# Edge blocks in pairs in the third and fifth segment of a round, and the root, scale and last step of y placed later

## The chip, the cores and the metric

The kernel runs on one core of a Trainium2 chip. The metric is the device time of one execution in microseconds, as the median of several runs. A core has five engines with an instruction queue each: TensorE (PE; its weight loads are shown apart as PEld), VectorE (DVE), ScalarE (ACT), GpSimd (POOL) and SyncE (SP), which here only issues transfers. They meet through semaphores.

## What is computed

A graph layer with 6,250 nodes, 206,250 edges and 128 features. The edges come sorted by their target node `dst`. Cut to what matters:

```python
h = x @ W_node.T + b_node
e = edge_attr @ W_edge.T + b_edge
msg = (h[src] + e) @ W_msg.T + b_msg
s = segment_sum(msg, dst)
y = x + s / max(deg, 1)
out = (y - mean(y)) / sqrt(var(y) + 1e-5)
```

Since all of it is linear up to the division, the kernel sums first and multiplies by the weights afterwards: for each node the sum of its edges' features and the sum of its sources' rows of x.

## The kernel before

**Two strands.** The first sums edge features. It reads `edge_attr` in 101 *blocks* of 2,048 edges (1 MB each) into three buffers `edges`. For a block TensorE multiplies one-hot rows of 32 relative targets with the edges (`sum_windows`, L545: 16 products of 128*32 tiles, each shown as two passes since it is f32, so 32 rows of the trace), which gives four windows of 32 nodes in `win_ps`. ScalarE copies them to `win_sb` (`copy_windows`, L1171), TensorE moves the four windows to their places with a product with `place` (`place_windows`, L552), and VectorE adds the result to `sums_e`, the sums of all nodes (`add_sums`, L744). `win_ps`, `win_sb` and `place` are double, `onehot` is threefold.

The second strand sums rows of x. For each of 25 groups of 250 nodes (a *round*) it counts how often each source occurs at each target. VectorE makes one-hot rows and keys (`make_hots`, L754), TensorE multiplies them (`count_fill`, L613), ScalarE moves the counts from three banks to `counts` (`move_bank`, L1227), and in the round after TensorE multiplies the counts with x, split in three bf16 parts (`apply_counts`, L628, 147 products a round).

**Slots, rounds, segments, fills.** All engines walk through the same 133 *slots*. The first 8 (the lead) hold one block each. Then come 25 rounds of 5 *segments*, each with 5 *fills* `f` = 0 to 4: on TensorE a fill is 5 count products and, from the second round on, some 6 products with x. The table `block_at` (L81 to L86) tells which block is summed in which slot: 93 blocks over the second to fifth segments of 25 rounds, one a segment at most. In a slot, TensorE does the block's windows first, then the fills, with the place product behind fill 1. VectorE makes the next segment's one-hots first, then adds the block of this segment, and makes `place` for the next block and `onehot` for the block after it. ScalarE copies the block's windows first and then moves the five banks.

**Finishing a group.** Two rounds after a group's counts were made, in the first segment of a round (`finish_at`), TensorE forms its message in `misc_ps` behind fill 3 (L639, L640). In the segment after, VectorE adds the residual (`add_message`, L793), the bias (L800), takes statistics (L807) and variance (L815), then the scale (`make_scale`, L820 and L822), for which ScalarE first gives the root (`take_root`, L1239, behind the move of fill 2). Another segment later ScalarE normalizes y (`normalize`, L1245) ahead of its moves.

**SyncE** issues everything in one queue. `load_edges(t)` (L378) waits until block t - 3 has been summed, since it fills that buffer; behind it, at fixed places in the order of blocks, come `load_resid` (L397) and `store` (L401), which waits for y.

**The start.** In the lead and the first two rounds VectorE and ScalarE also search the sorted targets for the places where nodes begin (`count_nodes` L849, `end_job` L856, `make_slots` L876, degrees L919); rounds can't be counted without them. `make_keys` (L768 to L783) prepares the next round's keys, TensorE turns them in the fourth segment.

## Time and profile before

| | us |
|---|---|
| median of 3 runs | 809.55 |
| lowest, highest | 808.64, 809.91 |
| profiled execution | 809.33 |
| its span, from first to last instruction | 807.5 |
| TensorE busy in it | 732.5 |
| VectorE busy | 634.8 |
| ScalarE busy | 462.2 |
| mean granted TensorE clock | 0.964 of full |

The granted clock has two levels, 2.4 GHz (1.00) and 1.2 GHz (0.50); a mean between them is a mixture over the stretch. An engine counts as busy while an instruction's modelled duration runs, and matmuls overlap, so a TensorE that is always busy may still have gaps between its weight loads. A time behind an arrow in square brackets is idle time before the row and what ended it; "issue" means that the profile shows nothing that ended it.

### The profile page before, as it was taken

To read this page: it belongs to the slowest core of one execution; us is meant where nothing else is said; L and a number is where in the kernel's file an instruction comes from. 1 tells how busy PE (TensorE), PEld (TensorE's weight loads), DVE (VectorE), ACT (ScalarE), POOL (GpSimd) and SP (SyncE) were. 2 spreads that over 40 slices of the span, in tenths; PEclk is the share of its full clock that TensorE was granted. 3 is DMA by queue.
4 is the path that set the end of the run, shared out by engine and by line. 5 is a ranking of instruction groups with operands and counts; after the bars stand their busy time and mean duration, and the time that the engine had idled before them with its cause. 6 is when DMAs were issued, how large, how long until landed. Compare 5 with 4: busy or idle time off the path is not lost.

```text
span 807.5 us, 24927 instructions
## 1 busy us (share of the span) xinstructions
PE 732.5 (91%) x10573; PEld 647.3 (80%) x10573; DVE 634.8 (79%) x1137; ACT 462.2 (57%) x948; POOL 80.5 (10%) x63
## 2 busy tenths in 40 slices
PE   2634569999999999999999999999999999999995
PEld 2423457888988898888988888898898889888895
DVE  7518997699878878887898788878887887888732
ACT  4104955575666566655666576566565656665641
POOL 2113722001000000000000000000000000000000
PEclk9995759899999999999999999999999999999998
DMA  6984426263446424644354454445534653364200
GB/s 206 215 278 156 141 68 179 84 196 122 137 146 223 144 97 162 207 143 162 115 190 151 163 175 125 158 147 197 171 105 134 218 158 130 113 220 134 98 14 16
DMA packets 71806, 121.11 MB, mean 150 GB/s; under 512 B 4717, under 2 KB 17738, under 8 KB 71591
## 3 DMA queue, kind: packets, MB, share of 16 engines
q1 hardware_dynamic: 68462, 115.72, 44.4%
q0 software_dynamic: 2496, 2.84, 1.5%
q8 instruction: 87, 1.43, 0.7%
q10 hardware_dynamic: 734, 0.90, 0.5%
q14 instruction: 27, 0.22, 0.1%
HBM read 116.19 MB, written 3.23 MB: 148 GB/s over the span
## 4 chain that ended last, share of the span: by engine, by line
PE 84%; DVE 8%; DMA 3%; issue 2%; SPq 2%; DVEq 0%; ACT 0%; ACTq 0%
PE x_ps L628 48%; PE count_ps L613 18%; PE win_ps L545 12%; PE win_ps L552 3%; DMA edges<-in_edge_attr_dram 2%; SPq L392 2%; DVE key_hot L754 1%; PE misc_ps L639 1%; PE misc_ps L640 1%; DVE row_hot L754 1%; DVE onehot L728 1%; DVE dve_junk L849 1%; DMA region<-in_dst_dram 1%; DVE region L827 1%; DVE place L734 1%
## 5 line engine op out<-in xcount | busy, mean ns | idle before, releaser
L628 PE MATMUL x_ps<-region,x_rest 128*128 128x250 bf16 x2450 | 450.3, 270 | 0.0
L1227 ACT CAST region<-count_ps 128x490 bf16<-128x490 f32 x625 | 350.8, 574 | 164.4 <-PE count_ps L613 158.8
L628 PE MATMUL x_ps<-region,x_hi 128*128 128x250 bf16 x1225 | 333.0, 272 | 0.0
L754 DVE TENSOR_TENSOR row_hot<-iota_bf,row 125x3200 bf16<-125x3200 bf16 x125 | 229.6, 1837 | 86.5 <-PE count_ps L613 59.7
L613 PE MATMUL count_ps<-key_hot,row_hot 125*128 125x98 bf16 x3125 | 244.7, 210 | 13.4 <-DVE key_hot L754 13.3
L628 PEld LDWEIGHTS x_ps<-region,x_rest 128*128 128x128 bf16 x2450 | 230.0, 98 | 17.7
L613 PEld LDWEIGHTS count_ps<-key_hot,row_hot 125*128 125x128 bf16 x3125 | 200.1, 99 | 43.0 <-issue 18.5
L754 DVE TENSOR_TENSOR key_hot<-iota_bf,key 125x2500 bf16<-125x2500 bf16 x125 | 183.2, 1466 | 0.0
L545 PE MATMUL win_ps<-edges,onehot 128*32 128x128 f32 x3232 | 119.2, 293 | 18.4 <-DMA edges<-in_edge_attr_dram 16.6
L628 PEld LDWEIGHTS x_ps<-region,x_hi 128*128 128x128 bf16 x1225 | 119.1, 97 | 8.0
L545 PEld LDWEIGHTS win_ps<-edges,onehot 128*32 128x32 f32 x3232 | 89.2, 116 | 40.6 <-issue 38.9
L477 POOL DMA_INDIRECT win_src<-in_src_dram,clipped_int x25 | 44.6, 1782 | 539.5 <-DVE key_bf L783 417.7
L1171 ACT COPY win_sb<-win_ps 128x128 f32<-128x128 f32 x101 | 26.9, 266 | 109.2 <-PE win_ps L545 106.4
L728 DVE TENSOR_TENSOR onehot<-iota_bf,rel_col 128x512 f32<-128x512 bf16 x101 | 72.1, 714 | 0.0
L552 PE MATMUL win_ps<-place,win_sb 128*128 128x128 f32 x202 | 43.7, 301 | 15.9 <-ACT win_sb L1171 11.0
L552 PEld LDWEIGHTS win_ps<-place,win_sb 128*128 128x128 f32 x202 | 32.8, 204 | 19.5 <-ACT win_sb L1171 12.6
L744 DVE TENSOR_TENSOR sums_e<-sums_e,win_ps 128x128 f32 x101 | 28.8, 285 | 13.9 <-PE win_ps L552 6.7
L734 DVE TENSOR_SCALAR place<-iota_f,pos 128x128 f32<-128x128 f32 x101 | 33.3, 329 | 0.0
L1239 ACT ACTIVATE stddev<-mean_var,eps_col 125x2 f32<-125x2 f32 x25 | 7.4, 296 | 35.9 <-DVE mean_var L815 35.9
L1245 ACT ACTIVATE y<-y,shift,rstd 125x128 f32<-125x128 f32 x50 | 22.0, 490 | 0.9 <-DVE shift L822 0.9
L793 DVE SCALAR_TENSOR_TENSOR y<-misc_ps,recip,resid 125x128 f32<-125x128 f32 x50 | 15.1, 344 | 8.9 <-PE misc_ps L640 8.9
L639 PE MATMUL misc_ps<-w_both,sums_e 128*125 128x128 f32 x100 | 19.2, 274 | 0.5 <-issue 0.5
(166 smaller groups left out, 345.0 us busy)
## 6 DMA issues: line engine op xcount, KB each, us to landing
edges<-in_edge_attr_dram SPq DMA_DIRECT2D x101, 1024.0 KB, 5.7
resid<-in_x_dram SPq DMA_DIRECT2D x25, 125.0 KB
out_dram<-y SPq DMA_DIRECT2D x25, 125.0 KB
region<-in_dst_dram ACTq DMA_DIRECT2D x1, 768.0 KB
win_src<-in_src_dram,clipped_int POOLq DMA_INDIRECT x25, 6.7
region<-in_L_gnn_W_node_dram SPq DMA_DIRECT2D x1, 64.0 KB
region<-in_L_gnn_W_edge_dram SPq DMA_DIRECT2D x1, 64.0 KB
region<-in_L_gnn_W_msg_dram SPq DMA_DIRECT2D x1, 64.0 KB
```

The source lines that it names most:

```text
L477: pool.indirect_dma_start(out=win_src[:, m % 3, :], out_offset=None, in_=src.rearrange("(r e) -> r e", e=WE), in_offset=bass.IndirectOffse ...
L545: mm = pe.matmul(bank[q * W:(q + 1) * W, 0:D], hot[:, q * J + j, :], edges[:, t % EDGE_SLOTS, q * J + j, :], start=(j == 0), stop=(j == J ...
L552: pe.matmul(l2_ps[t % 2], win_sb[:, t % 2, :], place[:, t % 2, :], start=True, stop=True).then_inc(l2_done, 1)
L613: mm = pe.matmul(count_ps[fill % COUNT_BANKS][:, k * KEYS:(k + 1) * KEYS], row_hot[0:WE, g % 2, f * FILL + k, :], key_hot[0:WE, g % 2, f * ...
L628: mm = pe.matmul(x_ps[m % 2][:, 0:NB], rows, counts[m % 2][:, b, :], start=(n == 0), stop=(n == PARTS - 1))
L639: pe.matmul(to, sums_e[:, first + h * PB:first + (h + 1) * PB], w_both[:, 1, :], start=True, stop=False)
L728: dve.tensor_tensor(onehot[:, t % ONEHOT_SLOTS, :, :], iota_bf[:, 0:W].rearrange("p (a w) -> p a w", a=1).to_broadcast([P, TILES, W]), rel ...
L734: dve.tensor_scalar(place[:, t % 2, :], iota_f[:, :], pos[:, sup_of[t]:sup_of[t] + 1], None, ALU.is_equal).then_inc(place_ready, 1)
L744: dve.tensor_tensor(to, to, l2_ps[t % 2], ALU.add).then_inc(added, 1)
L754: ins = dve.tensor_tensor(hot[0:WE, g % 2, :, :].rearrange("p w (a b) -> p w a b", b=4), iota_bf[0:WE, 0:width].rearrange("p (c a b) -> p ...
L1171: act.copy(win_sb[:, t % 2, :], win_ps[t % 2][:, 0:D]).then_inc(win_copied, 1)
L1227: act.copy(counts[m % 2][:, :, f * FILL * 2:(f + 1) * FILL * 2], count_ps[fill % COUNT_BANKS][:, 0:FILL * KEYS].rearrange("p (n b) -> p b ...
```

## The change

The table of blocks now holds lists. In the rounds blocks come two at a time, in the third and fifth segments (`s` = 2 and 4): 47 times over 50 places, so three of the places are left empty, and the last one holds one block. TensorE sums both blocks one after the other at the segment's start and puts both place products behind fill 1. ScalarE copies both windows first. VectorE adds both, then makes `place` and `onehot` for the next two. The lead is as before, but for a second `place` made at its end. There are still three edge buffers.

In the finish of a group the root moves from behind the move of fill 2 to behind that of fill 4; the scale moves from the end of its segment on VectorE to the next segment, behind its one-hots; and the last step of y moves from before the moves of that next segment to behind them.

```diff
--- before.py
+++ after.py
@@ -78,20 +78,22 @@
     SLOTS_B, SLOTS_A, DEGREES = 5, 8, 8
     group_of = [(G0 + m) % GROUPS for m in range(ROUNDS)]
     sup_of = [(FIRST + t) % NS for t in range(NS)]
-    block_at, blocks_by = [], [0]
+    PAIRS = -(-(NS - LEAD) // 2)
+    blocks_at, blocks_by = [], [0]
     for u in range(SLOTS):
         m, s = divmod(u - LEAD, SEGS)
-        due = u + 1 if u < LEAD else LEAD + -(-(NS - LEAD) * (m * (SEGS - 1) + s) // (ROUNDS * (SEGS - 1)))
-        block_at.append(blocks_by[-1] if due > blocks_by[-1] else None)
+        pairs = -(-PAIRS * (2 * m + (s >= 2) + (s >= 4)) // (2 * ROUNDS))
+        due = u + 1 if u < LEAD else min(NS, LEAD + 2 * pairs)
+        blocks_at.append(list(range(blocks_by[-1], due)))
         blocks_by.append(due)
-    slot_of = [block_at.index(t) for t in range(NS)]
-    assert blocks_by[-1] == NS
+    slot_of = [next(u for u in range(SLOTS) if t in blocks_at[u]) for t in range(NS)]
+    assert blocks_by[-1] == NS and max(len(ts) for ts in blocks_at) <= 2
 
 
     finish_slot = [LEAD + SEGS * (m + 2) if m < ROUNDS - 2 else SLOTS for m in range(ROUNDS)]
     finish_at = {u: m for m, u in enumerate(finish_slot) if u < SLOTS}
     summed_by = [blocks_by[u] for u in finish_slot]
-    assert not any(block_at[u] is not None for u in finish_at)
+    assert not any(blocks_at[u] for u in finish_at)
 
     LIMIT_B = (39.5, 3.7)
     LIMIT_A = (6.0, 3.7)
@@ -643,8 +645,8 @@
 
             pe.wait_ge(rel_copied, 2)
             for u in range(SLOTS):
-                t, g = block_at[u], u - LEAD
-                if t is not None:
+                g = u - LEAD
+                for t in blocks_at[u]:
                     sum_windows(t)
                 if u < LEAD:
                     if t in (0, 1):
@@ -661,7 +663,7 @@
                     count_fill(g, f)
                     if m > 0:
                         apply_counts(m - 1, s * FILLS + f, ROUND_FILLS)
-                    if f == 1 and t is not None:
+                    for t in blocks_at[u] if f == 1 else []:
                         place_windows(t)
                     if f == 2 and s == 3 and m + 1 < ROUNDS:
                         turn_keys(m + 1)
@@ -989,11 +991,15 @@
             make_onehot(1)
             block_counts(2)
 
+            placed, hot = [1], [2]
             for u in range(SLOTS):
-                t, g = block_at[u], u - LEAD
-                n = finish_at.get(u - 1)
+                ts, g = blocks_at[u], u - LEAD
+                t = ts[0] if ts else None
+                n, scaled = finish_at.get(u - 1), finish_at.get(u - 2)
                 if 0 <= g < SLOTS - LEAD - 1:
                     make_hots(g + 1)
+                if scaled is not None:
+                    make_scale(scaled)
                 if n is not None:
                     add_message(n)
                 if u < LEAD:
@@ -1010,22 +1016,22 @@
                         make_slots(0)
                     if t == 6:
                         make_keys(0)
-                if t is not None:
+                for t in ts:
                     add_sums(t)
                 if n is not None:
                     add_bias(n)
-                if t is not None and t + 1 < NS:
-                    make_place(t + 1)
+                while ts and placed[0] < min(NS, ts[-1] + 1 + (1 if u < LEAD - 1 else 2)):
+                    make_place(placed[0])
+                    placed[0] += 1
                 if n is not None:
                     take_stats(n)
-                if t is not None and t + 2 < NS:
-                    make_onehot(t + 2)
+                while ts and hot[0] < min(NS, ts[-1] + ONEHOT_SLOTS):
+                    make_onehot(hot[0])
+                    hot[0] += 1
                 if n is not None:
                     take_variance(n)
                 if u == LEAD - 1:
                     make_hots(0)
-                if n is not None:
-                    make_scale(n)
                 if g >= 0:
                     m, s = divmod(g, SEGS)
                     if s == (2 if m == 1 else 1) and m + 1 < ROUNDS:
@@ -1067,6 +1073,8 @@
             link(dve.tensor_reduce(totals[:, 1:2], l2_ps[0][0:1, 1:20], AX.X, ALU.add))
             link(dve.tensor_reduce(totals[:, 2:3], totals[:, 0:2], AX.X, ALU.add))
             dve.tensor_scalar(flag_int[:, :], totals[:, 2:3], 0.0, None, ALU.is_gt).then_inc(flag_ready, 1)
+            if SLOTS - 2 in finish_at:
+                make_scale(finish_at[SLOTS - 2])
             for n in (GROUPS - 2, GROUPS - 1):
                 add_message(n)
                 add_bias(n)
@@ -1251,10 +1259,10 @@
                 act.copy(rel_col[:, k * 8:(k + 1) * 8, :], count_ps[k][:, :].bitcast(BF16).rearrange("p (t c) -> p t c", t=8)[:, :, 0:NS]).then_inc(rel_copied, 1)
             roots, ends = 0, 0
             for u in range(SLOTS):
-                t, g = block_at[u], u - LEAD
+                g = u - LEAD
                 if g >= 0 and g % SEGS == 0 and g // SEGS >= 2:
                     take_x(g // SEGS - 2)
-                if t is not None:
+                for t in blocks_at[u]:
                     copy_windows(t)
                 if u < LEAD:
                     if t == 1:
@@ -1269,14 +1277,14 @@
                         spread_keys(0)
                     continue
                 m, s = divmod(g, SEGS)
-                if u - 2 in finish_at:
-                    normalize(ends)
-                    ends += 1
                 for f in range(FILLS):
                     move_bank(g * FILLS + f)
-                    if f == 2 and u - 1 in finish_at:
+                    if f == 4 and u - 1 in finish_at:
                         take_root(roots)
                         roots += 1
+                    if f == 4 and u - 2 in finish_at:
+                        normalize(ends)
+                        ends += 1
                     if f == 3 and s == 3 and m + 1 < ROUNDS:
                         spread_keys(m + 1)
                 if g < 2:
```

TensorE at the third segment of round 11, before. `edges` and `onehot` go in, `win_ps` comes out; `count_ps` is a count product, `x_ps` one with x:

```order
L628 MATMUL x_ps<-region,x_rest 128x250 x2
L628 MATMUL x_ps<-region,x_hi 128x250
L545 MATMUL win_ps<-edges,onehot 32x128 x16
L613 MATMUL count_ps<-key_hot,row_hot 128x98 x5
L628 MATMUL x_ps<-region,x_rest 128x250 x2
L628 MATMUL x_ps<-region,x_hi 128x250
```

And after the change, with its own line numbers, two higher:

```order
L630 MATMUL x_ps<-region,x_rest 128x250 x2
L630 MATMUL x_ps<-region,x_hi 128x250
L547 MATMUL win_ps<-edges,onehot 32x128 x32
L615 MATMUL count_ps<-key_hot,row_hot 128x98 x5
L630 MATMUL x_ps<-region,x_rest 128x250 x2
L630 MATMUL x_ps<-region,x_hi 128x250
```

The block of 16 products has become two blocks of 16 in a row.

VectorE in the second segment of the same round, behind the one-hots, before:

```order
L793 SCALAR_TENSOR_TENSOR y<-misc_ps,recip,resid 125x128 x2
L737 TENSOR_LOAD base_int
L737 ISA x2
L744 ISA
L744 TENSOR_TENSOR sums_e<-sums_e,win_ps 128x128
L800 SCALAR_TENSOR_TENSOR y<-bias_row,has_edge,y 125x128 x2
L734 TENSOR_SCALAR place<-iota_f,pos 128x128
L807 BN_STATS stats<-y 125x6 x2
L728 TENSOR_TENSOR onehot<-iota_bf,rel_col 128x512
L815 BN_AGGR mean_var<-stats 125x2 x2
L820 RECIPROCAL rstd<-stddev 125x2
L822 SCALAR_TENSOR_TENSOR shift<-mean_var,rstd 125x2
```

And after, from the statistics on (message and bias stand directly ahead of them), to the scale in the third segment:

```order
L809 BN_STATS stats<-y 125x6 x2
L817 BN_AGGR mean_var<-stats 125x2 x2
L770 TENSOR_SCALAR src_block<-win_src 125x125
L771 TENSOR_SCALAR past_mid<-iota_f,slot_mid 125x125
L772 TENSOR_SCALAR src_row<-win_src 125x125
L777 SCALAR_TENSOR_TENSOR past<-iota_f,slot_end,past_mid 125x125
L778 CAST row_bf<-src_row 125x125
L785 SCALAR_TENSOR_TENSOR key_bf<-past,src_block 125x125
L756 TENSOR_TENSOR row_hot<-iota_bf,row 125x3200
L756 TENSOR_TENSOR key_hot<-iota_bf,key 125x2500
L822 RECIPROCAL rstd<-stddev 125x2
L824 SCALAR_TENSOR_TENSOR shift<-mean_var,rstd 125x2
```

The block's add, place and one-hot have left this segment, the keys (from `src_block` to `key_bf`) follow the variance at once, and the scale stands behind the next segment's one-hots.

ScalarE, the same two segments, before:

```order
L1227 CAST region<-count_ps 128x49x10 x5
L1171 COPY win_sb<-win_ps 128x128
L1227 CAST region<-count_ps 128x49x10 x3
L1239 ACTIVATE stddev<-mean_var,eps_col 125x2
L1227 CAST region<-count_ps 128x49x10 x2
L1171 COPY win_sb<-win_ps 128x128
L1245 ACTIVATE y<-y,shift,rstd 125x128 x2
```

And after:

```order
L1235 CAST region<-count_ps 128x49x10 x10
L1247 ACTIVATE stddev<-mean_var,eps_col 125x2
L1179 COPY win_sb<-win_ps 128x128 x2
L1235 CAST region<-count_ps 128x49x10 x5
L1253 ACTIVATE y<-y,shift,rstd 125x128 x2
```

The root (`stddev`) stands behind both segments' ten moves, then two copies of windows come at once, and y is normalized behind five more moves.

## Rows read from the trace of the kernel before

**Rows 1.** The page: engines, then PEclk, the granted TensorE clock in 40 slices.

```profile
PE 732.5 (91%) x10573; PEld 647.3 (80%) x10573; DVE 634.8 (79%) x1137; ACT 462.2 (57%) x948; POOL 80.5 (10%) x63
...
PEclk9995759899999999999999999999999999999998
```

**Rows 2.** By stretches (us): busy us of each engine, granted clock, DMA share, GB/s.

```profile
142.00:147.00 5.00, 4.54 (x50) 3.34 (x51) 3.88 (x6) 1.20 (x3) 0.00 (x0) 0.50 0.02 3
400.00:600.00 200.00, 200.00 (x2983) 178.83 (x2980) 166.50 (x276) 122.89 (x250) 13.29 (x7) 1.00 0.47 154
405.00:409.00 4.00, 4.00 (x56) 3.56 (x57) 3.53 (x13) 1.68 (x5) 0.00 (x0) 1.00 0.82 259
```

**Rows 3.** Who waited for whom, 160 to 780 us: total us, times, longest us.

```profile
DVE row_hot L754 <- PE count_ps L613: 57.1, 44, 1.9
...
PEld win_ps L545 <- issue: 17.3, 84, 0.2
...
PEld count_ps L613 <- issue: 16.7, 84, 0.2
...
PE count_ps L613 <- DVE key_hot L754: 0.6, 1, 0.6
```

**Rows 4.** Weight loads on TensorE in order of time, 430 to 434 us: start, us, what.

```profile
430.61 0.10 PEld L628 LDWEIGHTS x_ps<-region,x_rest 128*128 128x128 bf16 x1
430.92 0.81 PEld L545 LDWEIGHTS win_ps<-edges,onehot 128*32 128x32 f32 x32 [0.21 <-issue]
431.93 0.25 PEld L613 LDWEIGHTS count_ps<-key_hot,row_hot 125*128 125x128 bf16 x5 [0.20 <-issue]
432.12 0.10 PEld L628 LDWEIGHTS x_ps<-region,x_rest 128*128 128x128 bf16 x1
...
432.60 0.10 PEld L628 LDWEIGHTS x_ps<-region,x_rest 128*128 128x128 bf16 x1
...
432.99 0.10 PEld L628 LDWEIGHTS x_ps<-region,x_rest 128*128 128x128 bf16 x1
...
433.57 0.30 PEld L552 LDWEIGHTS win_ps<-place,win_sb 128*128 128x128 f32 x2
433.79 0.30 PEld L613 LDWEIGHTS count_ps<-key_hot,row_hot 125*128 125x128 bf16 x4
```

**Rows 5.** The same view, 142 to 158 us: the gaps around a block at half clock.

```profile
144.57 1.48 PEld L545 LDWEIGHTS win_ps<-edges,onehot 128*32 128x32 f32 x32 [0.40 <-issue]
146.43 0.38 PEld L613 LDWEIGHTS count_ps<-key_hot,row_hot 125*128 125x128 bf16 x5 [0.38 <-issue]
```

**Rows 6.** SyncE's queue in order of time; landing times of edge loads, 200 to 750 us.

```profile
415.59 22.41 SPq L378 DMA_DIRECT2D edges<-in_edge_attr_dram  x4
...
443.32 22.41 SPq L378 DMA_DIRECT2D edges<-in_edge_attr_dram  x4
...
DMA to landing us min/median/max: 4.8/5.6/7.3
```

**Rows 7.** VectorE in order of time, the segment after a finished group, 402 to 413 us.

```profile
402.65 1.82 DVE L754 TENSOR_TENSOR row_hot<-iota_bf,row 125x3200 bf16<-125x3200 bf16 x1 [1.91 <-PE count_ps L613]
...
405.77 0.60 DVE L793 SCALAR_TENSOR_TENSOR y<-misc_ps,recip,resid 125x128 f32<-125x128 f32 x2
...
408.39 0.24 DVE L815 BATCH_NORM_AGGREGATE mean_var<-stats 125x2 f32<-125x6 f32 x2
...
409.28 0.23 DVE L768 TENSOR_SCALAR src_block<-win_src 125x125 int32<-125x125 int32 x1
```

**Rows 8.** VectorE in order of time, 119 to 146 us, before the steady part.

```profile
125.14 0.16 DVE L856 TENSOR_TENSOR job_rel<-job_cnt,job_off 125x4 f32<-125x4 f32 x1 [4.01 <-ACT act_junk L1185]
...
133.22 0.28 DVE L744 TENSOR_TENSOR sums_e<-sums_e,win_ps 128x128 f32 x1
...
134.22 0.22 DVE L768 TENSOR_SCALAR src_block<-win_src 125x125 int32<-125x125 int32 x1
...
139.62 0.17 DVE L876 COPY first_slot<-misc_ps 125x21 f32<-125x21 f32 x1
```

## Prediction

> **What bounds the kernel now.** I read the page's engine rows first, then the same by stretches of the span, then the waits of the long middle part, then single rows around an edge block. TensorE is busy 732.5 us of 807.5, VectorE 634.8. The page's clock line is uneven in its first ten slices and full after them [rows 1]. By stretches the division is clear: from 400 to 600 us TensorE is busy for all 200 us at the full granted clock, while VectorE works 166.5 of them [rows 2]. From 160 to 780 us VectorE waits 44 times, 57.1 us in all, for TensorE's count products, and TensorE waits for VectorE once, 0.6 us [rows 3]. So for 620 of 807 us the end is set by the sum of what TensorE issues, and a microsecond saved on ScalarE or VectorE there is worth nothing.
>
> Is anything of TensorE's time not work? "Busy" hides it, because the matmuls' modelled ends overlap; the weight loads show it. Before the first weight load of an edge block the load path stands still for 0.21 us, and before the first count product after the block for 0.20 us, both put down to "issue", that is, to nothing that the profile shows; there are 84 gaps of each kind in 620 us, 17.3 and 16.7 us in all [rows 3], one pair of gaps for every block.
>
> What does one block cost in TensorE's time? Take two passages from the last weight load of the x product to the first x load of the next fill [rows 4]. With a block between: 430.61 to 432.12, 1.51 us. Without: 432.60 to 432.99, 0.39 us. A block costs 1.12 us. Of this the 32 loads that carry it start within 0.81 less the last one's 0.11, so 0.70 us for 31 steps, 0.0226 us a step, 0.72 us for 32. The remaining 0.40 us is the crossing into the block and out of it.
>
> **Whose are the gaps?** Two readings. (a) They belong to the crossing between the full array (128*128) and the block's 128*32 tiles: the array runs empty, and it is paid once in, once out, however long the stay. (b) They belong to each block's own start, for instance its waits for four semaphores. The rows speak for (a), and I take it: at half clock (0.50 granted [rows 2]) the gaps are 0.40 and 0.38 us, twice as long, like the array's own work [rows 5]; and the gap behind the block stands before an ordinary count product, which has no gap in the fills that follow no block [rows 4].
>
> The Trainium skill, "TensorEngine Tiling (Array Packing)", section "Key Properties", says that changing the tiling mode, unlike changing the tile, drains TensorE. It would make the saving the full crossing for each pair. The Trainium skill, "Perfetto Trace Analysis", section "Optimization Strategy", says that a gap that keeps repeating on the engine that should be full can mean too few buffers. That would speak against this change, which keeps three edge buffers and asks for two at once: by it the gap would stay, as in rival C below. The trace has no releaser for any of the 84 gaps, and so agrees with the first page rather than the second.
>
> **The change part by part.**
>
> 1. *Pairs on TensorE.* The 93 blocks of the rounds become 46 pairs and one single block, the last. A pair pays one crossing: 1.12 + 0.72 = 1.84 us in place of 2.24, a saving of 0.40 us. The two place products stand together after the second fill; a place costs 433.79 - 433.57 = 0.22 us alone and has no gap [rows 4], so pairing them saves nothing. Pairs that count are those where TensorE sets the pace, from block 16 (round 2) on: blocks 16 to 99, 42 pairs. 42 x 0.40 = 16.8 us; bounds 0 (reading b) and 42 x 0.41 = 17.2 (both gaps in full). I take 16.6, since the join needs a semaphore check of which no row shows the price; nearest, the place product shows none.
>
> 2. *Edge loads.* A four-block round now lasts 443.32 - 415.59 = 27.73 us [rows 6]. Taking out four blocks and four places (4 x 1.34 = 5.36) leaves 22.4, some 4.5 us for a segment without a block, so 4.5 + 1.84 + 0.44 = 6.8 us for one with a pair. Of each pair the first block's end frees the buffer that the next pair's *second* block needs. From the third segment to the fifth that is 6.8 + 4.5 = 11.3 us. Loads land 4.8 to 7.3 us after issue, median 5.6 [rows 6]. Now a second load is issued 0.8 us behind the first. One load moves 1.05 MB, about 4.0 us at the 259 GB/s that one load reaches alone [rows 2]; were the two to share the engines evenly, the first would land after 5.6 + 4.0 = 9.6 us. That is still within 11.3. The cost is 0, and the cover is 1.7 us.
>
> 3. *VectorE.* Its work in a round stays the same; its place changes. One-hot rows for a segment take 405.77 - 402.65 = 3.1 us; message, bias, statistics and variance 408.63 - 405.77 less one block's 1.0 = 1.9; keys 1.3 (409.28 to 410.60, where the next one-hots began); a block's add, place and one-hot 134.22 - 133.22 = 1.0 [rows 7, 8]. Second segment: 3.1 + 1.9 + 1.3 = 6.3 against TensorE's 4.5, so 1.8 late into the third. There the next one-hots are ready at 1.8 + 3.1 = 4.9 of 6.8 us: 1.9 to spare. Then the scale (0.3) and two blocks' work (2.0): 7.2, 0.4 late. Fourth: one-hots at 3.5 of 4.5, and the fifth segment begins with a pair before it needs them. Fifth: 3.1, then the adds behind the places at about 3.9, end near 5.9 of 6.8. The lateness is gone before the round ends. Cost 0.
>
> 4. *Root, scale and last step of y.* Today the root waits for the variance in the middle of the moves; that wait is not on TensorE's path. In the new order the variance is there about 1.0 us earlier than 408.63, and ScalarE has done the segment's last move by about then; behind the root wait the copies of the pair in the next segment, which must wait for TensorE's first block anyway. The scale is no longer asked for behind its own root, so VectorE's short wait goes. The last step of y (0.9 us on ScalarE) ends near the end of the third segment. The store waits for it in SyncE's queue, and behind that store stands the load which waits for the first block of the fifth segment in any case. 0 on TensorE's path.
>
> 5. *The first 150 us.* From 70 to 150 us VectorE's order sets the pace: TensorE waits for its one-hots and tables. There the change puts a block's work behind the one-hots of the next segment: by the ninth segment VectorE has done two blocks less work ahead of the table step at 139.62 [rows 8], less what its 4.01 us wait for ScalarE's counts swallows [rows 8]. I make it 1.0 to 1.7 us earlier. TensorE then has the pair 14 and 15 in the segment at 144.57 rather than 15 alone: 0.72 + 0.22 more, or twice that at half clock, which rules there until 147 [rows 2, 5]. Net -0.7 to +0.9 us; and the slow stretch of about 5 us may be missed (-2.5) or last as long again (+2.5), since the idle time before it moves. I take -0.1.
>
> 6. *The end.* The last block comes a segment earlier, a single one, both ends as now. 0.
>
> **The sum.** The profiled execution took 809.33 us, its span 807.5, and 1.8 around it. 809.33 - 16.6 - 0.1 = 792.6. The median of the runs is 0.2 above the profiled one: 792.8 us.
>
> **Rivals.**
>
> A. *As summed*: 792.8, with the clock of the early part 790 to 796. For it: 84 equal gaps, doubled at half clock. 0.76.
>
> B. *Only one crossing is saved in a pair* (a new block still has to be started with its waits, 0.2 us): 42 x 0.2 = 8.4 saved, 801. Against it: the place product and the group's end have waits and no gap. 0.07.
>
> C. *The gaps stay, reading (b)*; the change doesn't give what its pairs are for: 809.4. Against it: the doubling at half clock. 0.05.
>
> D. *Slower: edge loads.* The second block of the fifth segment's pair waits for the load issued at the end of the third segment's first block. From 11.3 us of landing on it costs TensorE time, and from 11.3 + 16.7 / 20 = 12.1 us on the kernel is slower, as 20 rounds have both pairs. If two loads at once took twice the slowest landing, 14.6 us, each such wait would be 3.3: 66 us more, 859. Near its turning point it gives 811 to 815. For it: the trace has two loads in flight only in its noisy start. Against: 259 GB/s for one load uses the engines 0.82 [rows 2], and a round's mean need is unchanged. 0.06.
>
> E. *VectorE late*: if it is 2.2 us late rather than 1.8 after the second segment and its block work is slower too, TensorE waits up to 0.3 us in each of 22 rounds: 6.6 back, 799.4. Against: 1.9 us of spare. 0.06.
>
> **How the numbers follow.** The likeliest is A, 792.8. The range 789.5 to 801 takes A with its early bounds (792.8 - 2.5 - 0.8), E and B, together 0.89 by the cases, a little less for errors of my own. About 0.2% (1.6 us) is what a measurement of this kernel can tell from no change. Faster: A, B and E, 0.89. Same: C and a sliver of D, 0.06. Slower: 0.05.
>
> **What would show it.** In the waits of 160 to 780 us the gaps before blocks should be 43 rather than 84, near 8.8 us, and the same behind them. A pair should be 64 weight loads over about 1.53 us with no gap inside; a four-block round 26.9 us in SyncE's queue; the landing of edge loads 5.6 to 9.6 us and no wait of TensorE for them; the root's wait on ScalarE much below 34 us. The prediction is wrong if a gap stands inside the pairs, if TensorE waits for edges or one-hots in the fifth segment, or if the half-clock stretch near 145 us grows.

## The result

The changed kernel takes 800.52 us, median of four runs (798.70 to 801.85), where the kernel before takes 809.10 (808.51 to 809.91): the ratio is 0.9889, 95% interval 0.9867 to 0.9911, 8.6 us less. The forecast was 792.8 with a range of 789.5 to 801. The direction was right and the time lies just inside the range, but near its upper end: about half of what I had summed came. The profiled execution took 799.62 us, span 797.7. Two executions lay far above the others of their kernel and count in no ratio below: 882.04 us for one of the kernel before and 3810.98 us for one of the changed kernel, when it was run again.

The page of the changed kernel, engines and clock line, beside [rows 1]:

```profile
PE 716.8 (90%) x10573; PEld 649.6 (81%) x10573; DVE 640.0 (80%) x1137; ACT 467.9 (59%) x948; POOL 84.3 (11%) x63
...
PEclk9999979999999999999999999999999999999999
```

The waits from 160 to 770 us (who waited for what: us in total, times, longest), beside [rows 3]. The rows stand grouped by engine, and the first two are the crossings into and out of an edge block:

```profile
PEld win_ps L547 <- issue: 8.7, 42, 0.2
PEld count_ps L615 <- issue: 8.3, 42, 0.2
PEld count_ps L615 <- DVE key_hot L756: 3.9, 4, 1.7
...
PE count_ps L615 <- DVE key_hot L756: 2.8, 3, 1.5
...
DVE sums_e L746 <- DVE sums_e L746: 22.4, 42, 0.9
...
ACT stddev L1247 <- DVE mean_var L817: 9.9, 22, 1.5
```

The gaps are halved, 84 to 42 of each kind, 34.0 us to 17.0. That is what the change does, and all of it is there. Yet the time fell by 8.6 us and not by 17. In its place TensorE now waits 2.8 us for VectorE's one-hots, where it waited 0.6.

How long is a round? The first product of a group's message (`sums_e`) stands at the same place in every round. Before, in order of weight loads, in the first segments of rounds 2, 3 and 4 (rounds are numbered from 0):

```profile
154.97 0.30 PEld L639 LDWEIGHTS misc_ps<-w_both,sums_e 128*125 128x125 f32 x2
...
182.70 0.29 PEld L639 LDWEIGHTS misc_ps<-w_both,sums_e 128*125 128x125 f32 x2
...
209.85 0.30 PEld L639 LDWEIGHTS misc_ps<-w_both,sums_e 128*125 128x125 f32 x2
```

and after, in rounds 2, 3, 4 and 5:

```profile
152.89 0.30 PEld L641 LDWEIGHTS misc_ps<-w_both,sums_e 128*125 128x125 f32 x2
...
180.12 0.29 PEld L641 LDWEIGHTS misc_ps<-w_both,sums_e 128*125 128x125 f32 x2
...
209.10 0.30 PEld L641 LDWEIGHTS misc_ps<-w_both,sums_e 128*125 128x125 f32 x2
...
236.33 0.29 PEld L641 LDWEIGHTS misc_ps<-w_both,sums_e 128*125 128x125 f32 x2
```

A four-block round took 182.70 - 154.97 = 27.73 us and takes 180.12 - 152.89 = 27.23 us, and as much in every other round with two pairs to the end. Two pairs save 0.50 us, so one saves 0.25, not 0.40. Round 3, from 180.12 on, took 28.98, 1.75 too much. (My expectations below call this stall the one of round 2; it lies in round 3; of the four checks only the first runs at the end of round 2.) And the start came 2.1 us earlier in this execution.

Inside a pair, weight loads on TensorE in order of time, beside [rows 4]:

```profile
458.24 0.10 PEld L630 LDWEIGHTS x_ps<-region,x_hi 128*128 128x128 bf16 x1
458.54 1.69 PEld L547 LDWEIGHTS win_ps<-edges,onehot 128*32 128x32 f32 x64 [0.21 <-issue]
460.43 0.25 PEld L615 LDWEIGHTS count_ps<-key_hot,row_hot 125*128 125x128 bf16 x5 [0.20 <-issue]
460.62 0.14 PEld L630 LDWEIGHTS x_ps<-region,x_rest 128*128 128x128 bf16 x2
...
462.07 0.53 PEld L554 LDWEIGHTS win_ps<-place,win_sb 128*128 128x128 f32 x4
462.51 0.34 PEld L615 LDWEIGHTS count_ps<-key_hot,row_hot 125*128 125x128 bf16 x5
```

There is no gap between the two blocks: 64 loads in one row. But they take 1.69 us, not 1.53. From the last x load before to the first behind it is 460.62 - 458.24 = 2.38 us, less the 0.39 of a fill's start 1.99 us, where I had 1.84. The second block costs 0.88 us, and not 0.72. The four passes of two places take 462.51 - 462.07 = 0.44, twice 0.22, as forecast.

### The profile page after: what moved, and what is told of

Same layout as the page of the kernel before. It is cut to its first block, busy times and chain, and to the rows that moved or that the text cites. A ratio compares the mean times of both kernels' runs of the same rounds, so it can differ in the third digit from the quotient of the medians.

```text
span 797.7 us, 24927 instructions
## 1 busy us (share of the span) xinstructions
PE 716.8 (90%) x10573; PEld 649.6 (81%) x10573; DVE 640.0 (80%) x1137; ACT 467.9 (59%) x948; POOL 84.3 (11%) x63
## 4 chain that ended last, share of the span: by engine, by line
PE 75%; DVE 14%; issue 4%; DMA 4%; SPq 2%; DVEq 1%; ACT 0%; ACTq 0%
PE x_ps L630 44%; PE count_ps L615 15%; PE win_ps L547 10%; DVE key_hot L756 3%; DVE row_hot L756 3%; PE win_ps L554 3%; DMA edges<-in_edge_attr_dram 2%; SPq L394 2%; DVE onehot L730 1%; PE misc_ps L641 1%; PE misc_ps L642 1%; DVE dve_junk L851 1%; DVE place L736 1%; DMA region<-in_dst_dram 1%; DMA rows_words<-starts_dram 1%
## 5 line engine op out<-in xcount | busy, mean ns | idle before, releaser
L547 PE MATMUL win_ps<-edges,onehot 128*32 128x128 f32 x3232 | 108.7, 290 | 18.7 <-DMA edges<-in_edge_attr_dram 16.9
L547 PEld LDWEIGHTS win_ps<-edges,onehot 128*32 128x32 f32 x3232 | 91.4, 116 | 31.4 <-issue 29.8
L479 POOL DMA_INDIRECT win_src<-in_src_dram,clipped_int x25 | 47.8, 1910 | 528.1 <-DVE key_bf L785 406.6
L730 DVE TENSOR_TENSOR onehot<-iota_bf,rel_col 128x512 f32<-128x512 bf16 x101 | 68.4, 715 | 0.0
L554 PE MATMUL win_ps<-place,win_sb 128*128 128x128 f32 x202 | 35.4, 297 | 6.4 <-DVE place L736 4.1
L554 PEld LDWEIGHTS win_ps<-place,win_sb 128*128 128x128 f32 x202 | 29.0, 204 | 9.2 <-ACT win_sb L1179 4.5
L736 DVE TENSOR_SCALAR place<-iota_f,pos 128x128 f32<-128x128 f32 x101 | 30.4, 339 | 0.0
L1242 ACT COPY group_x<-x_ps 128x250 f32<-128x250 f32 x25 | 9.2, 369 | 18.2 <-PE x_ps L630 16.5
```

The costliest lines, as they stand in the source:

```text
L479: pool.indirect_dma_start(out=win_src[:, m % 3, :], out_offset=None, in_=src.rearrange("(r e) -> r e", e=WE), in_offset=bass.IndirectOffse ...
L547: mm = pe.matmul(bank[q * W:(q + 1) * W, 0:D], hot[:, q * J + j, :], edges[:, t % EDGE_SLOTS, q * J + j, :], start=(j == 0), stop=(j == J ...
L554: pe.matmul(l2_ps[t % 2], win_sb[:, t % 2, :], place[:, t % 2, :], start=True, stop=True).then_inc(l2_done, 1)
L730: dve.tensor_tensor(onehot[:, t % ONEHOT_SLOTS, :, :], iota_bf[:, 0:W].rearrange("p (a w) -> p a w", a=1).to_broadcast([P, TILES, W]), rel ...
L736: dve.tensor_scalar(place[:, t % 2, :], iota_f[:, :], pos[:, sup_of[t]:sup_of[t] + 1], None, ALU.is_equal).then_inc(place_ready, 1)
```

## The experiments

All ratios are to the kernel before, run beside it on the same chip.

### Is it the pairs or the finish?

Pairs alone: in the changed kernel the finish is put back.

```diff
-                if scaled is not None:
-                    make_scale(scaled)
...
+                if n is not None:
+                    make_scale(n)
...
+                if u - 2 in finish_at:
+                    normalize(ends)
...
-                    if f == 4 and u - 1 in finish_at:
+                    if f == 2 and u - 1 in finish_at:
                         take_root(roots)
```

> The changed kernel with the root, scale and last step of y put back where they were, so pairs alone. Theory (pairs do it all, the finish is off TensorE's path): 800 to 801 us, a four-block round still 27.2 us, gaps still 42 of each kind between 160 and 770 us. Rival (the finish had to move to make room for the pairs): ScalarE's wait for the variance and VectorE's for the root come back in the second segment, TensorE waits 0.3 us or more a round for one-hots or banks, 807 us or more.

Measured: 799.84 us, ratio 0.9896 (0.9869 to 0.9923). A four-block round is 27.23 us. The finish alone, on the kernel before (the same lines the other way round):

> The kernel before with only the root, scale and last step of y moved as in the change. Theory: no change, 809 to 810 us. Rival (the finish brings part of the 8.6 us by itself, for instance in the start): 807 or less.

Measured: 809.21 us beside 809.17, ratio 1.0005 (0.9992 to 1.0018); rounds of 27.73 us. So the pairs bring the gain, and the finish none of it. The waits of ScalarE for the variance with pairs and the old finish, 160 to 770 us:

```profile
ACT stddev L1245 <- DVE mean_var L817: 45.9, 23, 2.6
...
DVE rstd L822 <- ACT stddev L1245: 8.3, 23, 0.4
```

45.9 us of waiting, 36 more than in the changed kernel, cost a full round nothing: it takes 27.23 us in both. That three banks of counts cover some 2 us at a time is argued, not tried.

Beside pairs, the new place of the finish even costs a little. From the first message to the end of the span, the kernel with the old finish takes 797.9 - 154.03 = 643.87 us and the changed one 797.7 - 152.89 = 644.81. Three rounds make the difference: with the old finish round 3 takes 27.80 us and not 28.98, round 16 25.24 and not 25.87, but round 8 26.16 and not 25.40. Why round 3 differs stands below, with its stall.

### Is the saving the crossing?

The second block of each pair is summed behind the first fill, the places behind the third; all else, the loads and the order of the blocks too, is as in the changed kernel.

```diff
-                for t in blocks_at[u]:
+                for t in blocks_at[u][:1]:
                     sum_windows(t)
...
+                    for t in blocks_at[u][1:] if f == 0 else []:
+                        sum_windows(t)
-                    for t in blocks_at[u] if f == 1 else []:
+                    for t in blocks_at[u] if f == 2 else []:
                         place_windows(t)
```

> The changed kernel, but the second block of each pair is summed behind the first fill, and both places stand behind the third fill: same places in the rounds, same loads, a crossing more for every pair. Theory (what the pair saves is the crossing, 0.40 us, less a slower second block, 0.16 us): 84 gaps of each kind again, four-block round 27.7 us, time 42 x 0.25 = 10.5 us above the changed kernel, 810 to 812 us. Rival (the gain lies in the other order of VectorE's and ScalarE's work, not in the crossing): 800 to 802 us.

Measured: 814.51 us, ratio 1.0082 (1.0053 to 1.0111); 84 gaps before blocks, four-block rounds of 27.71 to 27.72 us. The crossing is the saving: with it back, the round is as long as before to 0.01 us. The time is 2.5 to 4.5 us above what I expected, and above the kernel before. Round 3 gives 2.4 of it, the start of the profiled execution (first message at 155.45 us) about as much. Weight loads of round 3 in order of time:

```profile
200.81 0.81 PEld L547 LDWEIGHTS win_ps<-edges,onehot 128*32 128x32 f32 x32 [0.21 <-issue]
204.31 0.25 PEld L615 LDWEIGHTS count_ps<-key_hot,row_hot 125*128 125x128 bf16 x5 [2.69 <-DVE key_hot L758]
...
205.90 1.48 PEld L547 LDWEIGHTS win_ps<-edges,onehot 128*32 128x32 f32 x32 [0.40 <-issue]
207.77 0.33 PEld L615 LDWEIGHTS count_ps<-key_hot,row_hot 125*128 125x128 bf16 x5 [0.38 <-issue]
```

TensorE stands still for 2.69 us before a count product, 0.20 of it the crossing and 2.49 the wait for one-hots; that they are late because the places, and with them VectorE's adds, come a fill later is argued. Then it runs at half speed for a while (granted clock 0.72 over 204 to 210 us): the next block takes 1.48 us with gaps of 0.40 and 0.38. With 0.16 us of waiting a segment earlier, the round took 31.87 us instead of 27.72, 4.15 for 2.65 of waiting.

### Why does the second block cost 0.88 us?

Two theories: the array's passes run at 27.5 ns and only the first ones behind a crossing run ahead; or the join, with its waits for four semaphores, costs 0.16 us. In the kernel before, each block's products are issued twice (and in a second kernel four times) into the same tile, without any wait between:

```diff
-                for j in range(J):
+                for j in [*range(J), *range(J)]:
                     for q in range(Q):
                         mm = pe.matmul(bank[q * W:(q + 1) * W, 0:D], hot[:, q * J + j, :], edges[:, t % EDGE_SLOTS, q * J + j, :],
```

> The kernel before with every block's 16 products issued twice in a row into the same tile, so 64 passes where there were 32, with no further wait or semaphore at the join and the same result. It measures the pace of the passes. Theory (after the first passes, which run ahead, the array takes 27.5 ns a pass): 64 loads in 1.69 us as in the pairs, 0.88 us more a block, 85 blocks in the steady part 75 us, 93 in the rounds 82, so 884 to 893 us. Rival (the passes run at 22.6 ns throughout, and the pair loses its 0.16 us to the waits at the join): 64 loads in 1.53 us, 0.72 us a block, 61 to 67 us, 870 to 877 us.

> The kernel before with every block's 16 products issued four times in a row into the same tile, 128 passes without a crossing, same result. It asks whether the pace found with two times holds. Theory (the loads at the entry run ahead once by 0.16 us, after that 27.5 ns a pass): 128 loads in 1.69 + 2 x 0.88 = 3.45 us, a four-block round 27.73 + 4 x 3 x 0.87 = 38.2 us. Rival (the pace keeps falling with the length of the stay, or rises again): 128 loads in more than 3.6 us or in less than 3.3.

Measured: 887.27 us twice, and 1053.78 us four times, this a single execution. The block's row at twice, and then at four times:

```profile
303.65 1.69 PEld L545 LDWEIGHTS win_ps<-edges,onehot 128*32 128x32 f32 x64 [0.21 <-issue]
```

```profile
446.95 3.43 PEld L545 LDWEIGHTS win_ps<-edges,onehot 128*32 128x32 f32 x128 [0.21 <-issue]
```

32 loads take 0.81 us [rows 4], 64 take 1.69, 128 take 3.43: 0.88 for the second 32 and 0.87 for each 32 after them. There is no wait at these joins, and they are just as long as the pair's. So the pair's join costs nothing. The pace is 27.2 to 27.5 ns a pass, and a stay of one block is 0.16 us shorter than its passes would be at that pace; the trace shows where: in the single block of the kernel before, as in the stays of 64 and 128, 8 loads have started after 0.1 us, and then come 4 in each 0.1 us for the most part. Why they may run ahead no run here shows. Joining two blocks gives this head start up once: 0.40 - 0.16 = 0.24 us a pair, and the rounds show 0.25. A four-block round with products four times takes 38.20 us, where 38.2 was expected. The whole time agrees: 887.27 is 78.1 us above the kernel before, between the 75 of the 85 blocks of the steady part and the 82 of all 93.

### What of the stall in round 3?

VectorE in the changed kernel, third segment of round 3, in order of time, beside [rows 7, 8]:

```profile
193.24 0.16 DVE L824 SCALAR_TENSOR_TENSOR shift<-mean_var,rstd 125x2 f32<-125x2 f32 x1
194.05 0.29 DVE L746 TENSOR_TENSOR sums_e<-sums_e,win_ps 128x128 f32 x1 [0.65 <-issue]
194.89 0.29 DVE L746 TENSOR_TENSOR sums_e<-sums_e,win_ps 128x128 f32 x1 [0.55 <-DVE sums_e L746]
195.09 0.47 DVE L736 TENSOR_SCALAR place<-iota_f,pos 128x128 f32<-128x128 f32 x2
195.48 1.29 DVE L730 TENSOR_TENSOR onehot<-iota_bf,rel_col 128x512 f32<-128x512 bf16 x2
196.69 0.26 DVE L897 TENSOR_SCALAR win_a<-rel_col 128x404 bf16<-128x404 bf16 x1
196.98 0.58 DVE L898 SCALAR_TENSOR_TENSOR win_a<-rel_col,win_a 128x404 bf16<-128x404 bf16 x1
...
197.80 1.82 DVE L756 TENSOR_TENSOR row_hot<-iota_bf,row 125x3200 bf16<-125x3200 bf16 x1
```

Between the scale, which ends at 193.40, and 196.69 stand the two blocks' operations, 3.3 us, not 2.0: with 0.65 us before the first add, put down to no releaser (the code reads the add's address there), and 0.55 before the second, which waits for the first and has an address of its own. Then one of four order checks, some 0.9 us (L897 to L900), which fall into just these segments.

The same place with pairs and the old finish, where no scale stands between the one-hots and the adds:

```profile
194.36 0.28 DVE L746 TENSOR_TENSOR sums_e<-sums_e,win_ps 128x128 f32 x1
194.85 0.29 DVE L746 TENSOR_TENSOR sums_e<-sums_e,win_ps 128x128 f32 x1 [0.21 <-DVE sums_e L746]
195.05 0.48 DVE L736 TENSOR_SCALAR place<-iota_f,pos 128x128 f32<-128x128 f32 x2
195.44 1.29 DVE L730 TENSOR_TENSOR onehot<-iota_bf,rel_col 128x512 f32<-128x512 bf16 x2
196.65 0.26 DVE L897 TENSOR_SCALAR win_a<-rel_col 128x404 bf16<-128x404 bf16 x1
```

Here the first add follows the one-hots (1.45 us) without idle time, the second 0.21 us behind it, and the two blocks take 2.3 us. So 1.0 of the 3.3 us comes with the short scale ahead of the adds; that the long one-hots hide the reading of the addresses is argued. Round 3 takes 27.80 us there: 0.57 too much and not 1.75.

TensorE's weight loads in the changed kernel, at the start of the fourth segment of round 3 and behind the pair of its fifth:

```profile
193.19 0.25 PEld L615 LDWEIGHTS count_ps<-key_hot,row_hot 125*128 125x128 bf16 x5 [0.31 <-DVE key_hot L756]
...
201.04 0.25 PEld L615 LDWEIGHTS count_ps<-key_hot,row_hot 125*128 125x128 bf16 x5 [1.73 <-DVE key_hot L756]
```

The checks are moved to the first segments of four later rounds:

```diff
-                    if 14 <= g < 18:
-                        check_order(g - 14)
-                    if g == 18:
+                    if g in (20, 25, 30, 35):
+                        check_order(g // 5 - 4)
+                    if g == 36:
                         dve.sem_inc(viol_ready, 1)
```

> The changed kernel with the four order checks of VectorE (0.9 us each, in four segments of round 2) moved to the first segments of rounds 4 to 7, where VectorE has time, the flag for them given later. Theory (VectorE was late in round 2 because the checks met a pair whose adds, place and one-hots take 3.3 us and not 2.0): round 2 takes 27.2 us instead of 29.0, TensorE's waits for one-hots from 160 us on go from 2.8 us to under 0.3, 1.75 us less than the changed kernel, 798 to 799.5 us. Rival (VectorE is late there with the pairs alone): the waits stay, 800 to 801 us.

Measured: 798.74 us, ratio 0.9887 (0.9857 to 0.9918). The messages of rounds 3 and 4:

```profile
180.67 0.29 PEld L641 LDWEIGHTS misc_ps<-w_both,sums_e 128*125 128x125 f32 x2
...
207.91 0.29 PEld L641 LDWEIGHTS misc_ps<-w_both,sums_e 128*125 128x125 f32 x2
```

Round 3 lasts 207.91 - 180.67 = 27.24 us: the 1.75 us are gone. TensorE still waits 1.3 us in all, which I had put under 0.3. These are the rounds with an empty place. In the changed kernel, weight loads in round 8 and in round 16:

```profile
329.05 0.25 PEld L615 LDWEIGHTS count_ps<-key_hot,row_hot 125*128 125x128 bf16 x5 [0.70 <-DVE key_hot L756]
...
552.34 0.25 PEld L615 LDWEIGHTS count_ps<-key_hot,row_hot 125*128 125x128 bf16 x5 [1.18 <-DVE key_hot L756]
```

The first stands behind the empty third segment of round 8, the second in the empty fifth of round 16. A segment without a pair, 4.5 us, is too short for VectorE to make up what the segment before left. That was in the table of blocks, and I had looked at full rounds only.

Next, one place and one one-hot go between the two adds:

```diff
                 for t in ts:
                     add_sums(t)
+                    if len(ts) == 2 and t == ts[0]:
+                        make_place(placed[0])
+                        placed[0] += 1
+                        make_onehot(hot[0])
+                        hot[0] += 1
```

> The changed kernel, but on VectorE one place and one one-hot stand between the two adds of a pair. Theory (0.55 us of the second add is waiting for the first, and VectorE sets the pace only in round 2): VectorE's 22 us of waiting of one add for the other go to under 3, the stall in round 2 shrinks from 1.75 by up to 1 us, 799.5 to 800.5 us in all. Rival (the pairs make VectorE late in many rounds): 797 us or less.

Measured: 799.06 us, ratio 0.9881 (0.9852 to 0.9909). VectorE's 22.4 us of waiting of one add for the other are gone from the list, and round 3 lasts 27.62 us instead of 28.98: the whole stall but 0.4. Round 16 takes 25.26 us instead of 25.87. That is more than I had expected, and the time lies below that theory's range, though not in the rival's. Both edits together:

> Both of these: order checks spread over rounds 4 to 7, and place and one-hot between the adds of a pair. Theory: as with the checks alone, since nothing waits for VectorE once the checks are gone, 798 to 799.5 us, no wait of TensorE for one-hots from 160 us on. Rival: the two add up, 797.5 us or less.

Measured: 798.66 us, ratio 0.9879 (0.9851 to 0.9907), the lowest median of this study, round 3 at 27.23 us. What TensorE waited for from 155 us on:

```profile
PE count_ps L615 <- DVE key_hot L756: 0.7, 2, 0.4
```

The 0.7 us stand against the expected none. By rows this version has 2.1 us less of waiting than the changed kernel. In the medians its interval covers the changed kernel's ratio, so "faster than the changed kernel" rests on the rows alone. With the old finish in this version:

> The changed kernel with the root, scale and last step of y where they were before, the order checks spread, and place and one-hot between a pair's adds. Theory (the place of the finish is worth nothing on TensorE's path, with pairs too): within 1 us of the version with the new finish, 798 to 800 us, four-block rounds 27.23 us. Rival (ScalarE's 2 us wait for the variance in each second segment is now close enough to hold up a bank): TensorE waits for ScalarE's moves from 160 us on, 801 us or more.

Measured: 800.29 us, ratio 0.9897 (0.9874 to 0.9919), four-block rounds 27.23 us. The time lies between the two expectations and doesn't decide; TensorE's waits do, 0.3 us in all for ScalarE's moves and 0.7 for one-hots. By the rounds the new finish is worth 0.5 us here: round 8 takes 25.40 us with it and 26.17 without, round 16 25.25 and 24.94. Beside plain pairs it cost 0.9, so its place is worth less than a microsecond either way.

### Was the early start a gain?

> The changed kernel with single blocks in rounds 0 and 1, placed as before, and pairs from round 2 on. Theory (the pairs' other order brought about 2 us at the start, 154.97 to 152.89 us at the first finished group): first finish again at 155 us, 802 to 803 us. Rival (those 2 us are scatter of the clock at the start): first finish anywhere between 152.5 and 155.5, time 799.5 to 801.5 us.

The edit: `LEAD + (4 * m + s if m < 2 else 2 * pairs)` in the table. Measured: 800.65 us, ratio 0.9910 (0.9881 to 0.9938). And the changed kernel itself once more:

> The changed kernel itself beside it on the same chip, to see how far its time and its first finished group (152.9 us before) scatter from run to run with nothing edited. Theory (the start's 2 us were scatter): 799 to 802.5 us, first finish between 152.5 and 157 us. Rival (the start gain is real): first finish within 0.3 us of 152.9.

Measured: 801.44 us, the median of five executions, ratio 0.9912 (0.9890 to 0.9934). The first message of the kernel with a single start, of the changed kernel again, and of the one with the checks spread, which does the same up to there:

```profile
152.99 0.29 PEld L641 LDWEIGHTS misc_ps<-w_both,sums_e 128*125 128x125 f32 x2
```

```profile
154.00 0.29 PEld L641 LDWEIGHTS misc_ps<-w_both,sums_e 128*125 128x125 f32 x2
```

```profile
153.44 0.30 PEld L641 LDWEIGHTS misc_ps<-w_both,sums_e 128*125 128x125 f32 x2
```

Single blocks at the start give 152.99 us, pairs 152.89, 154.00, 153.44 and, with the old finish, 154.03. The kernel before gave 154.97, and with the new finish alone, which does the same up to there, 154.11. So a kernel scatters by about 1 us against itself, and of the first comparison's 2.1 us at most 1 could be real. The spans speak against even that: the changed kernel's five here average 799.6 us, the ten of the kernel before beside them 807.0, 7.4 less, and from the first message to the end the profiled executions give 807.5 - 154.97 = 652.53 before and 799.2 - 154.00 = 645.20 for this one, 7.3 less. That leaves 0.1 us for the start.

VectorE's lead is lost there. The kernels with pairs in the first rounds wait for a transfer before a product with the turned slots (L579):

```profile
137.53 0.42 PEld L579 LDWEIGHTS misc_ps<-ident,rows_words 7*125 7x125 f32 x3 [3.42 <-DMA rows_words<-starts_dram]
```

The kernel before had no such wait there, and the one with single blocks at the start 0.57 us. That a VectorE that is ahead doesn't bring TensorE ahead fits this, but was not tried by itself.

## Why the prediction was right or wrong

**What bounds the kernel** was right: TensorE's own issue sets the pace in both, and what changed there is the time.

**Whose the gaps are** was right. They halved with the number of crossings, and came back when the pair was taken apart. The Trainium skill, "TensorEngine Tiling (Array Packing)", section "Key Properties", calls a change of mode a drain: the runs agree, 84 gaps to 42. A change of type or of the bank written is not enough for a gap: the place product is f32 too and writes `win_ps`, and has none [rows 4]. The block with full-width tiles was not run. The other page, "Perfetto Trace Analysis" of the Trainium skill, section "Optimization Strategy", which reads such a gap as a possible lack of buffers, doesn't apply here: the buffers stayed three and half of the gaps went.

**Part 1, the pairs: the failed term.** I took the second block at 32 x 22.6 = 72 hundredths of a us, from the starts of the loads within a single block. They start at 22.6 ns a pass there, because the first 8 start within 0.1 us; in a longer stay the pace is 27.2 to 27.5 ns. The second block costs 0.88 us, the pair saves 0.25 and not 0.40, and 42 pairs 10.5 us and not 16.6. My lower bound, 0, and the upper one held it; the value between was read from a stretch too short to be its own steady state.

**Part 2, the edge loads**, was right in its bound: landing 5.0, 7.1 and 9.5 us (least, median, most) where I had 9.6 for two that share the engines, against 470.80 - 459.68 = 11.1 us of room where I had 11.3, and no wait of TensorE for edges in the steady part. The median lies so far below because the 259 GB/s of [rows 2] are the mean of a whole load with its slow start: in its last two us, 407 to 409, it moved 408 and 383 GB/s, so a second load beside it adds less than 4.0 us. SyncE's queue and landing times (200 to 750 us), beside [rows 6]:

```profile
459.68 1.24 SPq L380 DMA_DIRECT2D edges<-in_edge_attr_dram  x2
...
466.15 0.30 SPq L403 DMA_DIRECT2D out_dram<-y  x1
470.80 1.26 SPq L380 DMA_DIRECT2D edges<-in_edge_attr_dram  x2
...
DMA to landing us min/median/max: 5.0/7.1/9.5
```

**Part 3, VectorE, was wrong by a term**: a block's work is 1.0 us when single, as it stands in [rows 8], and I put a pair's at 2.0. It is 2.3 us directly behind the one-hots and 3.3 behind the scale, where the changed kernel has it in the third segment. With "1.9 us to spare" this is harmless in a plain round, and there it was. It is not in round 3, with its checks (1.75 us), nor in rounds 8 and 16, which have an empty place (0.70 and 1.18 us before the load). I named VectorE's lateness as rival E, for each of 22 rounds, and it came in three. One of my signs of being wrong, a wait for one-hots in the fifth segment, came in rounds 3 and 16.

**Part 4** was right on ScalarE: the wait of the root is 9.9 us where it was 34. "0 on TensorE's path" missed the scale, whose new place makes the adds behind it dearer: with the old finish round 3 is 1.18 us shorter and round 16 0.63, against 0.76 more in round 8. **Part 5**, the start, was given as -0.1 us with wide bounds. The scatter covers it, and the wait for the transfer was not in it. **Part 6** holds: from the message of round 24 to the next one it is 28.29 us where it was 30.97, 2.68 less, as two blocks and places fewer should give.

The sum with the measured terms: -10.5 for 42 pairs; +1.75 for round 3; +1.7 for rounds 8 and 16, which took 25.40 and 25.87 us where 27.23 less a pair's 1.99 and two places' 0.44 would be 24.80; and -0.8, since the checks held up the kernel before too (its round 3, of three blocks, took 209.85 - 182.70 = 27.15 us, later ones of three 26.39). That is -7.8 us, 801.3; measured 800.5. Without the start, from the first message to the end, it is 652.53 us before and 644.81 after: -7.7. For the profiled executions, with 2.1 us of the start: -9.9, measured -9.7.

**The rivals.** The time fell between A (792.8) and B (801), near B, but not for B's reason: no gap remained in a pair. B reached the right place by a wrong mechanism, and only because it was there did the range hold the time; that is luck. C and D did not come.

## What to carry to other kernels

A switch of the array's tiles costs its gap once for each stay, so work of one tiling belongs together; but price the joined piece by the pace of a long stay, measured by doubling the work, not by the starts within a short one. Where work is bunched on the bounding engine, its followers are bunched too: look on them at the segments that have other work, and at the ones that a table leaves empty, rather than at the mean round. An engine that waits off the path (ScalarE, 45.9 us) can be left alone: moving the scale to spare it that put 1.0 us on VectorE in the third segment.

## What the runs showed of the hardware

- A crossing between 128*128 and 128*32 tiles showed as 0.21 us before and 0.20 us behind in each of 84 blocks, doubled at half clock; about 0.16 us of it is given back, as 8 loads start in the first 0.1 us. What one saves by avoiding a crossing was 0.25 us.
- The passes of the 128*32 tiles (128 columns, f32, two passes a product) took 27.2 to 27.5 ns each in stays of 64 and 128.
- Two adds in a row on VectorE, the second waiting for the first and reading its own address, had 0.21 us between them where the first stood directly behind the one-hots (1.45 us), and 0.53 to 0.56 elsewhere in full rounds; with two other operations between, no wait was left. An add directly behind the short scale had 0.65 us of idle time before it.
- In round 3 with pairs taken apart, TensorE waited 2.65 us and then ran a block at half speed (1.48 us instead of 0.81): the round took 4.15 us more.
- Two 1 MB loads issued some 0.9 us apart (1.24 us for both issues, 0.37 for one) landed after 7.1 us in the median and 9.5 at most; single ones after 5.6 and 7.3.
